# Local attention: where the mask is written and where the two parts of the rotation are summed

## The chip, the cores and the metric

The kernel runs on one core of a Trainium2 chip. The metric is the device time of one execution in microseconds (us). A core has TensorE (PE, matrix products), VectorE (DVE), ScalarE (ACT), GpSimd (POOL) and a queue for transfers (SP). Each works through its own instructions in order, and they wait for one another by semaphores.

## What is computed

The program is a stack of eight layers on a stream x of 8 x 256 tokens with 128 channels. The change is in the part called `ffn`, which stands in it twice. Each time it runs six pairs of a local attention and a gated feed-forward, so there are twelve local attentions. Cut to what matters:

```python
def attn_layer(x, Wqkv, qs, ksc, Wo):          # 16 heads of 64
    q, k, v = split(x @ Wqkv, 3)               # by heads
    q = l2norm(q) * qs;  k = l2norm(k) * ksc
    q = q * cos * scale + rotate_half(q) * sin * scale
    k = k * cos / scale + rotate_half(k) * sin / scale
    return local_attention(q, k, v) @ Wo
def local_attention(q, k, v):                  # windows of 32 queries
    sim = q @ concat(k_previous_window, k_own_window).T * 8
    sim = where(mask, -max, sim)               # 32 queries, 64 keys
    return softmax(sim) @ concat(v_previous_window, v_own_window)
```

The other layers of the stack (two attentions with other rules, a scan, a mixing layer) take the rest of the time; the change touches only names of semaphores there.

## The kernel before, in words

A local attention works on tiles of 128 tokens, 16 in a layer; two tiles are a unit (one sequence of 256 tokens), and a loop body has two units, so four tiles, tt = 0 to 3. Three bodies are a loop, the fourth is written out without the work for tiles that no longer exist. A layer starts with the projections of tiles 0 to 2 and the scores of tile 0.

All the order is written out by hand, one queue for each engine; in the body of tile tt each engine does work for tt and for the tiles ahead:

- **TensorE** (`fa_tensor`): products of x with `Wqkv` for tile tt+3, two banks at a time (L377), in turn with the transposes of q and k of tile tt+1 (`turn_qk`, L392 and L393): each 128x128 block is two transposing matmuls summed in PSUM, one of t1 (the cosine part) and one of t2 (the sine part), 32 a tile. Then the transposes of the probabilities of tt (L421), the first half of the scores of tt+1 (a bf16 matmul of the identity with the mask, L403, then 64 small matmuls on top of it, L408), the heads of tt (probabilities times values, 128 small matmuls, L434), the second half of the scores (again L403 and L408) and, in odd tiles, the projection by `Wo` (L446).
- **ScalarE** (`fa_scalar`): copies and squares of the banks of q, k and v (L499, L500, L502), the exponential of tile tt (`exps`, L525), the copies of the turned q and k (L520), then `rnorm` for tile tt+3 (L508, L510: one over the norm, by logarithm and exponential), the copy of the turned probabilities (`copy_probs`, L531), the copies of the heads (L539) and of the projection (L547). The copies of two banks of q and k stand ahead of the exponential, and `rnorm` stands ahead of `copy_probs`.
- **VectorE** (`fa_vector`): `softmax_norm` of tile tt (sum L600, reciprocal L602, product L606), `norms` of tile tt+3 (L611, L613), `unit_length` (L622, once for q, once for k: u = q or k over its norm), `softmax_shift` of tile tt+1 (maximum L592, difference L595), and in odd tiles the addition to the stream (L627).
- **GpSimd** (`fa_gpsimd`, `rotate`): for q and then for k, two half-width products of u with the sine table (L670, t2, the halves of each head swapped) and a product with the cosine table (L674, t1). It starts for a tile when the first L622 of that tile is done. t1 and t2 have two buffers each, by the parity of the tile.
- **SP** moves the values v into the layout of windows by small transfers.

What TensorE waits for in `heads`: the turned probabilities copied (L426). In `turn_qk`: both t1 and t2 of q (ahead of chunk 0) and of k (ahead of chunk 2), and a free bank. In `scores`: q and k copied out of PSUM, and the scores of the tile before read.

Of the kernel before, what the change touches and what calls it, by code (L numbers as in the profile page):

```python
# [8 lines left out]
BF16 = mybir.dt.bfloat16  # L9
ALU = mybir.AluOpType  # L10
# [104 lines left out]
def program(nc, d, out, parts=ALL):  # L115
    ctx = ExitStack()
    with ctx:
# [29 lines left out]
        ident_b = sb("ident_b", P, BF16)  # L147
        masks_b = sb("masks_b", 2 * 2 * WIN, BF16)
# [76 lines left out]
        masks_cast = sem("masks_cast")  # L225
# [141 lines left out]
        def fa_tensor(pe, run):  # L367
# [12 lines left out]
            def turn_qk(g, tt, chunks):  # L380
                t1, t2 = t1s[tt % 2], t2s[tt % 2]
                for c in chunks:
                    n = place_qk(tt, c)
                    pe.wait_ge(turned_copied, nth(g, TURN_PER, n))
                    if c % 2 == 0:
                        pe.wait_ge(t2_ready, nth(g, 2 * TILES, 2 * tt + c // 2) + 3)
                        pe.wait_ge(t1_ready, nth(g, 2 * TILES, 2 * tt + c // 2) + 3)
                    for j in range(4):

                        o = PS[:, TURN + n % 2, j * P:(j + 1) * P]  # L390
                        cols = slice((4 * c + j) * P, (4 * c + j + 1) * P)
                        pe.matmul(o, t1[:, cols], ident[:], start=True, stop=False, is_transpose=True)  # L392
                        last = pe.matmul(o, t2[:, cols], ident[:], start=False, stop=True, is_transpose=True)  # L393
                    last.then_inc(turned, 1)

            def scores(g, tt, s):
                uu, par = divmod(tt, 2)
                if s == 0:

                    wait_alone(pe, turned_copied, nth(g, TURN_PER, place_qk(tt, 3)) + 2)  # L400
                    wait_alone(pe, scores_read, nth(g, TILES, tt))
                mask = masks_b[:, par * 2 * WIN:(par + 1) * 2 * WIN].rearrange("p (o j) -> p o j", o=1)
                pe.matmul(PS[:, SCORE + s, :], ident_b[:], mask.broadcast_to([P, PAIRS, 2 * WIN]),  # L403
                          start=True, stop=False, skip_group_check=True)
# [74 lines left out]
        def fa_scalar(act, run):  # L479
# [46 lines left out]

            def copy_probs(g, tt, final):
# [21 lines left out]
            def body(g, it, final):  # L549
                for tt in range(TILES):  # L550
# [5 lines left out]
                    if ahead:  # L556
                        copy_turned(g, tt + 1, (0, 1))
# [16 lines left out]
            enter(1, 1)  # L574
            copy_qkv(first, 0, range(6), False)
# [8 lines left out]
            body(first + BODIES - 1, BODIES - 1, True)  # L584

        def fa_vector(dve, run):
# [36 lines left out]

            def add_stream(g, it, uu):
# [16 lines left out]
            for tt in range(3):  # L641
                norms(first, tt)
                unit_length(first, tt)
# [1597 lines left out]
```

## Time and profile before

| | before |
|---|---|
| times of three runs | 7197.66, 7207.6, 7215.52 us (median 7207.6) |
| profiled execution: own time, span | 7208.77 us, 7206.7 us |
| mean granted TensorE clock | 0.823 of full |
| busy: PE, DVE, ACT, POOL | 5312.7, 3840.9, 3985.0, 2396.7 us |
| L377 products with Wqkv (2304) | 1163.5 us busy |
| L408 scores, L434 heads (24576 each) | 451.1 and 534.7 us busy |
| L392, L393 transposes (6144 in all) | 1399.3 us busy, overlapping |
| L403 mask matmuls (384) | 149.3 us busy |
| L670, L674 products of GpSimd (768, 384) | 1152.7 and 938.5 us busy |

How to read it: the busy time of an engine is a sum over its instructions, and pipelined matmuls overlap, so the distance between the starts of two of them says more than the duration of one. The span runs from the first to the last instruction; the execution's own time holds 2.1 us more. Busy shares average over layers with different limits; within a stretch, the timeline shows which engine waits for which. An idle time in brackets stands behind the instruction that ended it, with its releaser. The local attentions lie between 873 and 3080 us and between 3947 and 6200 us of the span, in turn with their feed-forwards.

### The profile page before, as it was taken

The page shows a single profiled execution, that of the slowest core. Times are in us where ns is not written, and L with a number is a line of the kernel's source. Part 1 is how long each engine was busy: PE and PEld are TensorE (multiplying, and loading weights), DVE is VectorE, ACT ScalarE, POOL GpSimd, SP SyncE. Part 2 cuts the span into 40 slices and gives each one's busy share as a digit, 9 for nine tenths or more (in the row PEclk, how much of TensorE's full clock was granted, in tenths as well). Part 3 has the DMA queues.
Part 4 walks back from the last instruction along what each step waited for, and adds up shares of the span by engine and source line. Part 5 has one row for each costly group of instructions (what it writes and reads, how often), then busy time and mean ns, then how long its engine had stood idle before and what let it go on. Part 6 is the DMA issues. An engine that isn't in the chain of part 4 may idle for free. (4 is left out here: it accounts for less than half of the span.)

```text
span 7206.7 us, 178920 instructions
## 1 busy us (share of the span) xinstructions
PE 5312.7 (74%) x69288; PEld 3368.6 (47%) x69288; DVE 3840.9 (53%) x6202; ACT 3985.0 (55%) x8451; POOL 2396.7 (33%) x1351
## 2 busy tenths in 40 slices
PE   1000198888888888977777988888888979687778
PEld 0000065655656564733333655656564747343444
DVE  5555654645455554555554645455554546445854
ACT  4333264646455555539997646555554546355655
POOL 0000162626354444504443626354453535000000
PEclk6555599999999999976666989999998989766876
DMA  1000121212222121200000212212121212000000
GB/s 43 0 0 0 37 51 48 55 49 54 53 49 59 42 53 50 57 11 1 1 1 20 55 47 53 54 45 52 47 57 44 57 45 57 18 2 3 0 2 6
DMA packets 177838, 248.52 MB, mean 34 GB/s; under 512 B 51692, under 2 KB 79848, under 8 KB 175080
## 3 DMA queue, kind: packets, MB, share of 16 engines
q1 hardware_dynamic: 177128, 237.68, 13.2%
q8 instruction: 613, 10.04, 0.6%
q14 instruction: 97, 0.79, 0.0%
HBM read 43.50 MB, written 5.24 MB: 7 GB/s over the span
## 5 line engine op out<-in xcount | busy, mean ns | idle before, releaser
L377 PE MATMUL PS<-arena 128*128 128x512 f32 x2304 | 1163.5, 632 | 220.0 <-ACT arena L500 117.1
L670 POOL TENSOR_TENSOR arena<-arena 128x512 f32<-128x512 f32 x384 | 586.6, 1551 | 651.3 <-DVE arena L622 651.3
L670 POOL TENSOR_TENSOR lns<-arena 128x512 f32<-128x512 f32 x384 | 566.1, 1498 | 666.7 <-DVE arena L622 666.7
L377 PEld LDWEIGHTS PS<-arena 128*128 128x128 f32 x2304 | 412.9, 199 | 646.1 <-issue 359.7
L499 ACT ACTIVATE arena<-PS 128x512 f32<-128x512 f32 x768 | 472.1, 615 | 333.4 <-PE PS L377 258.4
L434 PE MATMUL PS<-arena 64*64 64x32 f32 x24576 | 534.7, 227 | 155.4 <-ACT arena L531 121.4
L592 DVE TENSOR_REDUCE arena<-PS 128x16 f32<-128x1024 f32 x192 | 235.2, 1225 | 731.0 <-PE PS L408 731.0
L1106 PE MATMUL PS<-arena 128*128 128x512 f32 x8 | 6.7, 1019 | 807.8 <-DVE arena L1040 807.8
L434 PEld LDWEIGHTS PS<-arena 64*64 64x64 f32 x24576 | 509.5, 141 | 191.7 <-issue 188.0
L611 DVE TENSOR_REDUCE arena<-arena 128x32 f32<-128x2048 f32 x192 | 438.8, 2285 | 293.4 <-ACT arena L500 286.1
L539 ACT ACTIVATE arena<-PS 128x512 f32<-128x512 f32 x384 | 208.9, 597 | 648.0 <-PE PS L434 648.0
L622 DVE TENSOR_TENSOR arena<-arena 128x1024 f32<-128x1024 f32 x384 | 471.7, 1270 | 148.4 <-ACT arena L510 148.4
L674 POOL TENSOR_TENSOR arena<-arena 128x1024 f32<-128x1024 f32 x192 | 482.3, 2512 | 0.0
L500 ACT ACTIVATE arena<-PS 128x512 f32<-128x512 f32 x768 | 476.4, 620 | 0.0
L408 PE MATMUL PS<-arena 64*32 64x64 f32 x24576 | 451.1, 218 | 31.3 <-issue 29.1
L520 ACT ACTIVATE arena<-PS 128x512 f32<-128x512 f32 x768 | 435.0, 634 | 49.7 <-PE PS L393 49.7
L2040 POOL TENSOR_TENSOR arena<-arena 128x1024 f32<-128x1024 f32 x128 | 297.9, 2356 | 477.6 <-ACT arena L1889 477.6
L674 POOL TENSOR_TENSOR lnc<-arena 128x1024 f32<-128x1024 f32 x192 | 456.2, 2376 | 0.0
L408 PEld LDWEIGHTS PS<-arena 64*32 64x32 f32 x24576 | 376.1, 107 | 148.7 <-issue 148.1
L1799 PE MATMUL PS<-arena 32*128 32x512 f32 x768 | 324.8, 968 | 163.6 <-DVE arena L1947 133.3
L600 DVE TENSOR_REDUCE arena<-arena 128x16 f32<-128x1024 f32 x192 | 234.3, 1220 | 316.2 <-ACT arena L525 316.2
L446 PE MATMUL PS<-arena 128*128 128x256 f32 x1536 | 385.5, 406 | 8.2 <-ACT arena L539 8.2
(254 smaller groups left out, 11101.2 us busy)
## 6 DMA issues: line engine op xcount, KB each, us to landing
arena<-arena SPq DMA_DIRECT2D x2880, 64.0 KB, 2.0
arena<-in_L_ffn_Wqkv SPq DMA_DIRECT2D x12, 1536.0 KB, 6.5
arena<-in_L_ffn_Wo SPq DMA_DIRECT2D x48, 128.0 KB, 6.3
scratch<-arena SPq DMA_DIRECT2D x4, 1024.0 KB, 4.8
arena<-scratch SPq DMA_DIRECT2D x4, 1024.0 KB, 7.6
arena<-in_L_ffn_W SPq DMA_DIRECT2D x12, 341.0 KB
arena<-in_ffn_scales SPq DMA_DIRECT2D x12, 128.0 KB, 5.8
arena<-in_L_ffn_W SPq DMA_DIRECT2D x12, 128.0 KB
```

Of the source, the lines that this page charges most:

```text
L377: pe.matmul(PS[:, QKV + n % 2, :], xs[uu % 2][:, par * P:(par + 1) * P], w, start=True, stop=True).then_inc(qkv_ready, 1)
L408: last = pe.matmul(PS[w * WIN:(w + 1) * WIN, SCORE + s, m * FD:(m + 1) * FD], qT[s * FD:(s + 1) * FD, m, w * WIN:(w + 1) * WIN], KT[uu % 2 ...
L434: last = pe.matmul(PS[(m % 2) * FD:(m % 2 + 1) * FD, HEAD + head_index(tt, s) % 2, at:at + WIN], VW[par][rows, w, m * FD:(m + 1) * FD], PT ...
L446: last = pe.matmul(PS[:, HEAD + n % 2, 0:T], Wo[:, m, :], AT[uu][:, m, :], start=(m == 0), stop=(m == PAIRS - 1))
L499: act.activation(chunk(raws[tt % 2], c), bank, ACT.Copy)
L500: act.activation(chunk(sq, c), bank, ACT.Square).then_inc(qkv_copied, 1)
L520: act.activation(to, PS[:, TURN + n % 2, :].rearrange("p (m t) -> p m t", m=4), ACT.Copy)\
L611: dve.tensor_reduce(nrm[:, 3, :], h3(sq), AX_X, ALU.add).then_inc(norm2_own, 1)
L622: dve.tensor_tensor(h3(raw[:, part]), h3(raw[:, part]), rn, ALU.mult).then_inc(u_ready, 1)
L670: last = pool.tensor_tensor(heads(t2)[:, :, a:a + 32], heads(raws[par])[:, :, b:b + 32], sine, ALU.mult)
L674: pool.tensor_tensor(heads(t1), heads(raws[par]), cosine, ALU.mult).then_inc(t1_ready, 1)
L1799: last = pe.matmul(PS[:, 2 * k + s, :], b0_KM[n % 2][rows_of(s), kt * P:(kt + 1) * P], b0_qb[(par + i // CHUNKS) % 2][rows_of(s), :, qt * ...
```

## The change

1. ScalarE writes the mask, broadcast over the 16 heads, into both score banks (`write_mask`, one activation of 128x1024) behind the exponential of the tile before; the scores are summed on top of it. The two mask matmuls of a tile and the bf16 copies of identity and mask go. At the start of a layer TensorE claims the two banks with one fp32 matmul each (`banks_marked`), and ScalarE waits for them.
2. The sine table holds its halves swapped, so GpSimd makes t2 with one full-width product per q and k instead of two halves. t2 now has its halves in u's order, and the swap is done where t1 and t2 are added.
3. t1 and t2 are added ahead of the transposes: q by VectorE (`rotate_q`, two additions of 128x512, of tile tt+2, between `softmax_norm` and `norms`), k by GpSimd (two additions of 128x512 behind its products, after a wait for them). TensorE transposes the sum: 16 single transposes a tile, after `q_rotated` and `k_rotated`.
4. In the first attention of the stack three semaphores are merged into others.

```diff
 def turn_qk(g, tt, chunks):
...
-                    if c % 2 == 0:
-                        pe.wait_ge(t2_ready, nth(g, 2 * TILES, 2 * tt + c // 2) + 3)
-                        pe.wait_ge(t1_ready, nth(g, 2 * TILES, 2 * tt + c // 2) + 3)
+                    if c == 0:
+                        pe.wait_ge(q_rotated, nth(g, TILES, tt))
+                    if c == 2:
+                        pe.wait_ge(k_rotated, nth(g, TILES, tt))
                     for j in range(4):
-                        pe.matmul(o, t1[:, cols], ident[:], start=True, stop=False, is_transpose=True)
-                        last = pe.matmul(o, t2[:, cols], ident[:], start=False, stop=True, is_transpose=True)
+                        last = pe.transpose(PS[:, TURN + n % 2, j * P:(j + 1) * P], t1[:, cols], ident[:])
 def scores(g, tt, s):
...
-                    wait_alone(pe, scores_read, nth(g, TILES, tt))
-                pe.matmul(PS[:, SCORE + s, :], ident_b[:], mask.broadcast_to([P, PAIRS, 2 * WIN]),
-                          start=True, stop=False, skip_group_check=True)
+                    wait_alone(pe, mask_ready, nth(g, TILES, tt))
 fa_tensor, ahead of the first qkv of a layer:
+            for s in range(2):
+                pe.matmul(PS[:, SCORE + s, :], ident[:], Wqkv[:, 0:CH], start=True, stop=True).then_inc(banks_marked, 1)
 fa_scalar:
+            def write_mask(g, tt):
+                S = PS[:, SCORE:SCORE + 2, :].rearrange("p s (m e) -> p (s m) e", e=FD)
+                act.activation(S, masks[:, tt % 2:tt % 2 + 1, :].broadcast_to([P, FH, 2 * WIN]), ACT.Copy)\
+                   .then_inc(mask_ready, 1)
...
                     exps(g, tt)
                     if ahead:
+                        write_mask(g, tt + 1)
                         copy_turned(g, tt + 1, (0, 1))
...
+            act.wait_ge(banks_marked, 2 * (run + 1))
+            write_mask(first, 0)
             copy_qkv(first, 0, range(6), False)
+        def add_halves(eng, t1, t2, k):
+            heads = lambda a: a[:, k * INNER:(k + 1) * INNER].rearrange("p (h e) -> p h e", e=FD)
+            for half in range(2):
+                a, b = half * 32, 32 - half * 32
+                last = eng.tensor_tensor(heads(t1)[:, :, a:a + 32], heads(t1)[:, :, a:a + 32],
+                                         heads(t2)[:, :, b:b + 32], ALU.add)
+            return last
 fa_vector:
+            def rotate_q(g, tt):
+                dve.wait_ge(t2_ready, nth(g, 2 * TILES, 2 * tt) + 3)
+                dve.wait_ge(t1_ready, nth(g, 2 * TILES, 2 * tt) + 3)
+                add_halves(dve, t1s[tt % 2], t2s[tt % 2], 0).then_inc(q_rotated, 1)
...
                     softmax_norm(g, tt, nth(g, TURN_PER, place_probs(tt - 1, 1, False)))
+                    if not (final and tt + 2 >= TILES):
+                        rotate_q(g, tt + 2)
                     if not (final and tt + 3 >= TILES):
                         norms(g, tt + 3)
                         unit_length(g, tt + 3)
...
             for tt in range(3):
                 norms(first, tt)
                 unit_length(first, tt)
+                if tt == 1:
+                    rotate_q(first, 0)
             softmax_shift(first, 0)
+            rotate_q(first, 1)
 fa_gpsimd, rotate (the table's halves are swapped where it is made):
-                    for half in range(2):
-                        a, b = half * 32, 32 - half * 32
-                        sine = table[:, 2 + k, par:par + 1, a:a + 32].broadcast_to([P, FH, 32])
-                        last = pool.tensor_tensor(heads(t2)[:, :, a:a + 32], heads(raws[par])[:, :, b:b + 32], sine,
-                                                  ALU.mult)
-                    last.then_inc(t2_ready, 1)
+                    sine = table[:, 2 + k, par:par + 1, :].broadcast_to([P, FH, FD])
+                    pool.tensor_tensor(heads(t2), heads(raws[par]), sine, ALU.mult).then_inc(t2_ready, 1)
...
+                wait_alone(pool, t2_ready, nth(g, 2 * TILES, 2 * tt + 1) + 3)
+                wait_alone(pool, t1_ready, nth(g, 2 * TILES, 2 * tt + 1) + 3)
+                add_halves(pool, t1s[par], t2s[par], 1).then_inc(k_rotated, 1)
```

## Rows read from the trace of the kernel before

**Rows 1.** Windows: an odd tile, then an even one; columns as in the first line.

```profile
core 0: us, PE busy (x) PEld busy (x) DVE busy (x) ACT busy (x) POOL busy (x), PEclk, DMA share, GB/s
1345.07:1365.04 19.97, 18.81 (x330) 14.14 (x327) 12.50 (x11) 11.12 (x22) 14.37 (x9) 1.00 0.26 62
1365.04:1381.12 16.08, 15.11 (x310) 11.13 (x311) 10.11 (x8) 11.44 (x23) 6.82 (x5) 1.00 0.22 53
```

**Rows 2.** Timeline of the even tile, TensorE: start, duration, instruction, idle before.

```profile
1365.04 1.98 PE L377 MATMUL PS<-arena 128*128 128x512 f32 x4 [0.49 <-issue]
...
1373.78 1.04 PE L421 MATMUL PS<-ident,arena 128*128 128x128 f32 x8
1374.66 0.38 PE L403 MATMUL PS<-masks_b,ident_b 128*128 128x512 bf16 x1
1374.97 1.10 PE L408 MATMUL PS<-arena 64*32 64x64 f32 x64
1376.61 2.52 PE L434 MATMUL PS<-arena 64*64 64x32 f32 x128 [0.55 <-ACT arena L531]
```

**Rows 3.** Waits: who, for whom, us in total, times, longest us.

```profile
PE PS L434 <- ACT arena L531: 121.4, 168, 1.6
```

**Rows 4.** Timeline of the even tile, ScalarE.

```profile
1368.12 1.08 ACT L525 ACTIVATE arena<-arena 128x1024 f32<-128x1024 f32 x1
...
1374.71 0.23 ACT L508 ACTIVATE arena<-arena 128x32 f32<-128x32 f32 x1
...
1375.20 1.06 ACT L531 ACTIVATE arena<-PS 128x512 f32<-128x512 f32 x2
```

**Rows 5.** Timeline, VectorE: L606 of the odd tile, then the even tile.

```profile
1351.04 1.30 DVE L606 TENSOR_TENSOR arena<-arena 128x1024 f32<-128x1024 f32 x1
...
1370.88 1.23 DVE L606 TENSOR_TENSOR arena<-arena 128x1024 f32<-128x1024 f32 x1
1372.17 2.29 DVE L611 TENSOR_REDUCE arena<-arena 128x32 f32<-128x2048 f32 x1
```

**Rows 6.** Groups by line (busy us, mean ns); last a single L670 in time.

```profile
L674 POOL TENSOR_TENSOR lnc<-arena 128x1024 f32<-128x1024 f32 x192 | 456.2, 2376 | 0.0
L333 DVE TENSOR_TENSOR XN<-lnc,lns 128x512 f32<-128x512 f32 x72 | 49.8, 692 | 45.1 <-ACT lns L324 45.1
...
1277.96 1.29 POOL L670 TENSOR_TENSOR lns<-arena 128x512 f32<-128x512 f32 x1
```

**Rows 7.** Timeline of a layer's start, VectorE and GpSimd, one instruction each.

```profile
1271.92 1.64 DVE L622 TENSOR_TENSOR arena<-arena 128x1024 f32<-128x1024 f32 x1 [0.65 <-ACT arena L510]
1272.44 2.27 POOL L670 TENSOR_TENSOR arena<-arena 128x512 f32<-128x512 f32 x1
1273.49 2.31 DVE L622 TENSOR_TENSOR arena<-arena 128x1024 f32<-128x1024 f32 x1
1274.68 3.32 POOL L674 TENSOR_TENSOR arena<-arena 128x1024 f32<-128x1024 f32 x1
```

**Rows 8.** Timeline, GpSimd: first and last products that run into the odd tile.

```profile
1340.65 3.42 POOL L670 TENSOR_TENSOR lns<-arena 128x512 f32<-128x512 f32 x2 [8.09 <-DVE arena L622]
...
1348.87 2.39 POOL L674 TENSOR_TENSOR lnc<-arena 128x1024 f32<-128x1024 f32 x1
```

**Rows 9.** Timeline of the same layer's start: TensorE, GpSimd, VectorE.

```profile
1253.79 4.58 PE L377 MATMUL PS<-arena 128*128 128x512 f32 x6 [8.39 <-issue]
...
1285.31 2.37 POOL L674 TENSOR_TENSOR lnc<-arena 128x1024 f32<-128x1024 f32 x1
...
1298.81 2.35 DVE L606 TENSOR_TENSOR arena<-arena 128x1024 f32<-128x1024 f32 x1
```

**Rows 10.** Two pauses of TensorE (timeline), and a window behind the second.

```profile
1562.29 4.28 PE L434 MATMUL PS<-arena 64*64 64x32 f32 x128 [0.97 <-ACT arena L531]
...
1587.88 4.51 PE L716 MATMUL PS<-XN,arena 128*128 128x512 f32 x6 [4.37 <-DVE XN L336]
...
1588.00:1589.00 1.00, 1.00 (x2) 0.43 (x3) 0.00 (x0) 0.00 (x0) 0.00 (x0) 0.71 0.00 0
```

More of the change, by code:

```diff
@@ L224, in program @@
         probs_ready = sem("probs_ready")
-        masks_cast = sem("masks_cast")
+        mask_ready = sem("mask_ready")
+        q_rotated = sem("q_rotated")
+        k_rotated = sem("k_rotated")
+        banks_marked = sem("banks_marked")
         vw_ready = [sem(f"vw_ready{i}") for i in range(2)]
@@ L380, in turn_qk @@
             def turn_qk(g, tt, chunks):
-                t1, t2 = t1s[tt % 2], t2s[tt % 2]
+                t1 = t1s[tt % 2]
                 for c in chunks:
@@ L651, in fa_gpsimd @@
             pool.wait_ge(attn_w_loaded, (run + 1) * ATTN_LOADS)
-            for k in range(4):
-                last = pool.tensor_tensor(table[:, k, :, :], rotary[:, k, :, :],
-                                          qks[:, k:k + 1, :].broadcast_to([P, 2, FD]), ALU.mult)
+            for k in range(2):
+                pool.tensor_tensor(table[:, k, :, :], rotary[:, k, :, :],
+                                   qks[:, k:k + 1, :].broadcast_to([P, 2, FD]), ALU.mult)
+            for k in range(2, 4):
+                for half in range(2):
+                    a, b = half * 32, 32 - half * 32
+                    last = pool.tensor_tensor(table[:, k, :, b:b + 32], rotary[:, k, :, a:a + 32],
+                                              qks[:, k:k + 1, a:a + 32].broadcast_to([P, 2, 32]), ALU.mult)
             last.then_inc(tables_ready, 1)
@@ L894, in program @@
         s_mix = sem("s_mix")
-        s_sh = sem("s_sh")
         s_rest = sem("s_rest")
@@ L937, in a0_sync @@
             sp.dma_start(a0_R.rearrange("p (b t) -> p b t", b=B), scratch[3].rearrange("b c t -> c b t"))\
-              .then_inc(s_backed, 16)
+              .then_inc(s_back, 16)
         def a0_vector(dve, n0):
@@ L947, in a0_vector @@
             dve.tensor_copy(a0_sh.rearrange("p (b t) -> p b t", t=T)[:, :, 1:T],
-                            XN[:].rearrange("p (b t) -> p b t", t=T)[:, :, 0:T - 1]).then_inc(s_sh, 1)
-            dve.wait_ge(s_sh, 1)
+                            XN[:].rearrange("p (b t) -> p b t", t=T)[:, :, 0:T - 1]).then_inc(s_rest, 1)
+            dve.wait_ge(s_rest, 3)
             for k in range(4):
@@ L1035, in a0_vector @@
                .then_inc(s_stat, 1)
-            dve.wait_ge(s_rstd, 2)
+            dve.wait_ge(s_rn, 4)
             dve.tensor_scalar(a0_tmp, a0_tmp, a0_small[:, 40:41], a0_small[:, 43:44], ALU.subtract, ALU.mult)\
                .then_inc(s_wkv, 1)
-            dve.wait_ge(s_backed, 16)
+            dve.wait_ge(s_back, 32)
             dve.tensor_scalar(a0_R, a0_R, a0_vec[:, 9:10], a0_vec[:, 10:11], ALU.mult, ALU.add).then_inc(s_gn, 1)
@@ L1088, in a0_scalar @@
             act.wait_ge(s_stat, 9)
-            act.activation(a0_small[:, 42:43], a0_small[:, 41:42], ACT.Ln, bias=eps[:, 0:1]).then_inc(s_rstd, 1)
-            act.wait_ge(s_rstd, 1)
-            act.activation(a0_small[:, 43:44], a0_small[:, 42:43], ACT.Exp, scale=-0.5).then_inc(s_rstd, 1)
+            act.activation(a0_small[:, 42:43], a0_small[:, 41:42], ACT.Ln, bias=eps[:, 0:1]).then_inc(s_rn, 1)
+            act.wait_ge(s_rn, 3)
+            act.activation(a0_small[:, 43:44], a0_small[:, 42:43], ACT.Exp, scale=-0.5).then_inc(s_rn, 1)
         def a0_tensor(pe, n0):
```

8 lines of the change are left out of this document (removed).

## The prediction

> **What bounds the kernel now.** I read the stretches by window first. The attention layers (12 of them, 16 tiles of 128 tokens each, 192 tiles) repeat a pair of tiles: an odd one, which also projects, of 19.97 us and an even one of 16.08 us, with TensorE busy 18.81 and 15.11 us of them at full clock [rows 1]. That looks like TensorE as the bound, and the change takes work from TensorE. So the question is what TensorE waits for in the rest. Its order of time for an even tile, counted as t from its first qkv matmul at 1365.04, shows one wait that counts: 0.55 us before the 128 head matmuls of L434, released by ScalarE's copy of the turned probabilities, L531 [rows 2]. The table of waits has the same pair 168 times in the 192 tiles [rows 3].
>
> Then I follow that wait back. L531 stands behind the two small activations of rnorm in ScalarE's own queue: L508 at 1374.71, L531 at 1375.20 [rows 4]. L508 needs the norms that VectorE makes with L611 (1372.17, 2.29 us), and L611 stands right behind L606 (1370.88, 1.23 us) with no idle time between them [rows 5]. L606 follows from the exponential, which ScalarE starts at 1368.12, after its four copies of the new qkv banks. So there is a ring: first qkv matmuls, copies, exponential (t = 3.1), sums and L606 (ends t = 7.1), L611 (ends t = 9.4), rnorm, L531, heads (t = 11.6), scores, next tile. VectorE and ScalarE set its length; the transposes of q and k lie beside it. TensorE has only 0.55 us of slack against it, and no piece of the ring has any.
>
> **The change part by part.**
>
> Transposes, 32 to 16. The eight transposes of L421 take 1373.78 to 1374.66, 0.11 us each, so 1.76 us of TensorE go per tile [rows 2]. They lie ahead of the wait at L434: worth nothing while the ring stands, since the wait grows by as much.
>
> Mask matmuls. Each holds TensorE 0.31 us (1374.66 to 1374.97) [rows 2]. The one of the first half lies ahead of the same wait, worth nothing. The one of the second half stands between heads and scores, on the ring: -0.3 us in every tile.
>
> The mask by ScalarE. No row shows a copy from SBUF to PSUM; the nearest is the exponential of the same 128x1024, 1.08 us [rows 4]. I take 1.1, bounds 0.9 and 1.4. It is queued behind the exponential and ahead of the copies of the turned q and k and of the next qkv banks, so TensorE gets its banks 1.1 us later. Today ScalarE goes from L502 into L508 with no idle time listed for L508 [rows 4], so this would be paid. It is hidden only because VectorE is later still (next item); if that cover were gone it would cost up to 1.1.
>
> VectorE's two additions for q. They come between L606 and L611, in the ring. A 128x512 with two SBUF inputs takes 0.69 us [rows 6]; the pair, overlapping a little, 1.35; bounds 1.2 without waits and, with a wait for a GpSimd instruction of 2.37 ahead of each, 6. Queued behind them are L611 and both L622, and ScalarE's L508 and L531 wait for L611.
>
> GpSimd. The two half-width sine products become one of 2.37 us, the duration of the cosine product, and two half-width additions of k of 1.29 are added [rows 6]: 4 x 2.37 + 2 x 1.29 = 12.1 us a tile where there were 2 x 2.37 + 4 x 1.29 = 9.9 without waits. Its throughput is enough (a pair of tiles has 36 us). But GpSimd and VectorE exclude each other. The rows of the prologue show it: L622 starts at 1271.92 and takes 1.64 instead of 1.23, because L670 is running; L670 then takes 2.27, the next L622 2.31, the next L674 3.32 [rows 7]. Each lasts its own time plus that of the other's: when both have work, they alternate, instruction by instruction.
>
> The Trainium skill (SBUF — State Buffer, "SBUF: two separate sides") says the same of the pair of ports that the two share, an exclusive lock for a whole instruction. It does not say who is next when both stand waiting; were VectorE always to keep the pair for its next instruction, the sum below would be that of the second case, 7400. The rows say alternate, so I go by them.
>
> Where they meet, **odd tile** (t from 1345.07): GpSimd's turn of a tile begins at 1340.65, and its last product, 1348.87 with 2.39, ends at 1351.26 [rows 8], just as L606 begins (1351.04, 1.30 long [rows 5]), t = 6.0 to 7.3. The cut of 0.2 to 0.4 in the sine products and the 0.3 that the next tile comes earlier cancel: the end of the last product stays at t = 6.1 to 6.3. From there GpSimd now has two additions. L606 runs first, to 7.3; addition one of k to 8.6; first half of q (waiting since 7.3) to 9.3; addition two of k to 10.5; second half of q to 11.2. L611 starts at 11.1 instead of 7.3: +3.8, -0.3 for the mask: +3.5 us.
>
> **Even tile:** GpSimd's turn begins at the same place of the tile ahead, but that tile is 3.9 us longer behind this place, for its projection [rows 1]. Without a meeting the turn ends at t = 6.2 + 2.6 = 8.8 in an odd tile, so here at 4.9, or 5.4 with the stream addition of VectorE in between; L606 starts at 5.8 [rows 5]. No meeting, by a margin of 0.4 us: +1.35 - 0.3 = +1.0.
>
> **Start of a layer.** Two fp32 matmuls that claim the score banks are put ahead of the first qkv. That stretch begins when weights and inputs are there, and six passes take 4.58 us, 0.76 each [rows 9]; four more are 3.1 us at that pace. A passage of the four products of one bank at full clock takes less (1.98 us for four [rows 2]), so an earlier start of TensorE may give part back: +2 (bounds 1 and 3.1). Then GpSimd, which works without a pause until 1287.7 (1285.31 plus 2.37) [rows 9] for two tiles, now needs 2 x 2.2 more for these and waits for the additions and L622s of VectorE that fall between (some 4.5, an estimate from their durations), and frees itself at about 1296.6. The addition for tile 1 stands ahead of the first softmax_norm and waits for GpSimd twice (+4); L606 of tile 0, which today takes 2.35 because of such a wait [rows 9], and the addition for tile 2 wait again (+4). I take +8 for the first tile, bounds +2 and +10.
>
> **Last three tiles** of a layer make no norms, so the ring isn't there; a mask matmul each: -1 in all.
>
> Sum for a layer: 2 + 8 + 6 x 1.0 + 6 x 3.5 - 1 = 36 us; 12 layers: 432. The renamed semaphores of the first attention and the two casts that go add nothing: they are the same waits under other names, and off the ring. The profiled execution took 7208.8 us (span 7206.7), 1 us over the median of the three runs, so 7208.8 + 432 = 7641; forecast 7640.
>
> **The rivals.**
>
> *Second case, the additions meet no GpSimd work, or VectorE goes first.* For it: in the even tile the two miss each other, and a shift of 1.5 us would do so in the odd one. Against: L606 already ends on GpSimd's last product. Each tile then +1.0, the first +3: 2 + 3 + 6 + 6 - 1 = 16 a layer, 192, so 7400.
>
> *Third case, the clock.* In an odd tile TensorE would stand idle some 4.5 us ahead of the heads. A pause of 4.37 us elsewhere was followed by a granted clock of 0.71 in the next microsecond, on the way from 2.4 to 1.2 GHz [rows 10]; after a longer one the heads took 4.28 us instead of 2.52 [rows 10, 2], 1.8 more, and the second scores and the projection follow at that clock. 1.7 to 4.8 us for 72 odd tiles: 7760 to 7985. Against: the clock is 1.00 through both tiles now [rows 1], and the pause lies between stretches of dense work. The Trainium skill (TensorE: Matmul & The Clock Gate, "Part 4: PE-mode transpose") has it that transposes don't count as activity for the clock gate; then the 16 that go cost no clock, and what is left of this case is the pause alone.
>
> *Fourth case, faster.* Place: the wait at L434. If it were not the ring that ends it, but a nearly finished TensorE, every tile would shrink by 1.76 + 0.62 = 2.38 us: 192 x 2.38 = 457, so 6752. It decides if the chain from the exponential to L531 has 1.35 us to spare. Against it: L606 and L611 touch, L508 comes 0.2 us after L611, L531 right behind. A part of it could give no change or a few per cent less.
>
> That the change doesn't do what it says is hardly possible: the instructions are written out one by one.
>
> **How the numbers follow.** Forecast 0.50 (7540 to 7760 by its bounds), second case 0.22 (7330 to 7540), third 0.17, fourth 0.08, and 0.03 for costs and gains that cancel. 7640 is the likeliest's own. The range 7330 to 7860 takes in the first two and the near half of the third. 0.3% is 22 us, about what a measurement can tell from no change; faster by more 0.08, within 0.03, slower by more 0.89.
>
> **What would show it.** Right: L611 starts 1.35 us or more behind the end of L606; the wait PE L434 behind ACT L531 grows from 0.55 to some 2 us in even and 4 to 5 in odd tiles; VectorE's additions and GpSimd's show durations well over 0.69 and 1.29 in odd tiles; tile pairs of 40 to 41 us instead of 36.05. Second case: pairs of 38. Wrong: pairs under 36, L434 without a wait. Third: granted clock under 1.00 in the middle of layers.

## The result, and the profile after

The changed kernel takes 7875.4 us (median of 4 runs, 7851.52 to 7899.01) where the kernel before takes 7211.56 on the same chips: a ratio of 1.0919 (95% interval 1.0876 to 1.0962). It is slower, by 664 us. The forecast was 7640 in a range of 7330 to 7860. The profiled execution has a span of 7897.2 us against 7206.7.

From the page of the changed kernel, busy times and then the granted clock in 40 slices (line numbers of the changed kernel from here on; the heads are L430 now, the scores L404, the products with `Wqkv` L378, the copy of the probabilities L536, the norms L628, `softmax_norm`'s product L623, the additions L599 on both engines):

```profile
PE 5524.5 (70%) x65880; PEld 3414.2 (43%) x65880; DVE 4239.3 (54%) x6586; ACT 4148.9 (53%) x8643; POOL 2883.4 (37%) x1371
...
PEclk5555787878788888886666877788887887766776
```

TensorE runs 3408 matmuls fewer and is busy for 212 us longer. The second line says why: most slices of the attention layers that had 9 before have 7 or 8 now. The windows of an even tile, the odd one behind it, and ten microseconds in the middle of that odd one:

```profile
1403.77:1420.76 16.99, 13.17 (x294) 8.84 (x292) 11.76 (x11) 12.56 (x25) 9.66 (x6) 1.00 0.20 50
1420.76:1447.42 26.66, 21.48 (x308) 16.00 (x309) 14.83 (x13) 11.58 (x22) 21.34 (x11) 0.81 0.23 54
1436.00:1446.00 10.00, 10.00 (x198) 8.87 (x195) 3.19 (x3) 1.09 (x2) 9.92 (x4) 0.51 0.17 39
```

Against [rows 1] the even tile is 0.9 us longer at full clock, and the odd one 6.7 us, with a stretch at half clock. TensorE in order of time through both:

```profile
1413.70 1.10 PE L404 MATMUL PS<-arena 64*32 64x64 f32 x64
1416.27 2.52 PE L430 MATMUL PS<-arena 64*64 64x32 f32 x128 [1.47 <-ACT arena L536]
...
1420.76 1.98 PE L378 MATMUL PS<-arena 128*128 128x512 f32 x4 [0.94 <-ACT arena L482]
...
1435.66 3.90 PE L430 MATMUL PS<-arena 64*64 64x32 f32 x128 [3.63 <-ACT arena L536]
1439.48 1.93 PE L404 MATMUL PS<-arena 64*32 64x64 f32 x64
1441.34 6.24 PE L442 MATMUL PS<-arena 128*128 128x256 f32 x16
```

The wait ahead of the heads was 0.55 us [rows 2]; it is 1.47 in the even and 3.63 in the odd tile. Behind the long one the clock falls, and the heads take 3.90 instead of 2.52, the scores 1.93 instead of 1.10, the projection 6.24 instead of 3.73 (both shorter durations stand in e2 below). The table of waits has 168 waits as in [rows 3], 2.6 times as long in all:

```profile
PE PS L430 <- ACT arena L536: 319.5, 168, 3.8
```

Why the odd tile's wait is long: VectorE first, one instruction each, then GpSimd.

```profile
1426.73 1.23 DVE L623 TENSOR_TENSOR arena<-arena 128x1024 f32<-128x1024 f32 x1
1427.87 1.76 DVE L599 TENSOR_TENSOR lnc<-lnc,lns 128x512 f32<-128x512 f32 x1
1429.55 1.76 DVE L599 TENSOR_TENSOR lnc<-lnc,lns 128x512 f32<-128x512 f32 x1
1431.24 2.27 DVE L628 TENSOR_REDUCE arena<-arena 128x32 f32<-128x2048 f32 x1
...
1426.72 2.36 POOL L599 TENSOR_TENSOR lnc<-lnc,lns 128x512 f32<-128x512 f32 x1 [0.17 <-POOL lnc L703]
1429.04 1.73 POOL L599 TENSOR_TENSOR lnc<-lnc,lns 128x512 f32<-128x512 f32 x1
```

The additions of VectorE need some 0.69 us each [rows 6] and last 1.76; those of GpSimd need 1.29 and last 2.36 and 1.73. They alternate as in [rows 7]: L623 holds GpSimd's first addition up, which holds VectorE's first one up, and so on. L628 starts at t = 10.5 where L611 started at 7.3.

In the even tile they don't meet. There L628 starts at t = 8.1, and one row of ScalarE shows how close a second bound is, the square of the last q and k bank, which L628 also needs:

```profile
1411.85 2.28 DVE L628 TENSOR_REDUCE arena<-arena 128x32 f32<-128x2048 f32 x1
...
1411.05 0.67 ACT L499 ACTIVATE arena<-PS 128x512 f32<-128x512 f32 x1
```

It ends at 1411.72, 0.1 us ahead of L628. ScalarE's queue has the mask in it, so without VectorE's additions, 1.3 us long, L628 could start only 0.1 us earlier.

The odd tile above is not the common one. The next pair of tiles in the same layer, heads of the even tile, VectorE's additions in the odd one, heads of the odd one:

```profile
1459.95 4.17 PE L430 MATMUL PS<-arena 64*64 64x32 f32 x128 [1.50 <-ACT arena L536]
...
1474.87 1.29 DVE L599 TENSOR_TENSOR lnc<-lnc,lns 128x512 f32<-128x512 f32 x2
...
1480.49 4.22 PE L430 MATMUL PS<-arena 64*64 64x32 f32 x128 [1.47 <-ACT arena L536]
```

Here the even tile's clock falls behind a wait of 1.50 us, and in the odd one the additions meet nothing, the wait is 1.47, and the clock falls all the same. Of the 72 odd tiles 28 stand behind an even tile at full clock: there the pair of additions takes 2.35 to 3.46 us, the wait is 3.16 to 3.76 us, and the clock falls in all 28. The other 44 stand behind a tile with a fall: the pair takes 1.29 us, the wait is 1.47 to 1.66, and the clock falls in 30 of them.

**Account by stage.** For each trace I took the 16 starts of the exponential in each of the 12 attention layers, and the time at the lower clock between the first and the thirteenth. A layer's start is counted from GpSimd's first product of the rotation's table, which waits for the layer's weights. Means of the 12 layers, in us:

| kernel | first table product to exp 0 | exp 0 to 1 | exp 1 to 12 | exp 12 to 15 | half clock, exp 0 to 12 |
|---|---|---|---|---|---|
| before | 47.5 | 18.2 | 198.4 | 46.4 | 2.8 |
| changed | 48.2 | 27.6 | 240.2 | 50.8 | 93.0 |
| e2, pause filled | 48.1 | 25.6 | 222.8 | 50.5 | 13.3 |
| e3, mask alone | 47.7 | 19.0 | 210.9 | 50.5 | 13.4 |
| e4, sums alone | 46.6 | 28.8 | 242.3 | 54.5 | 96.1 |
| e1, q behind norms | 48.3 | 24.0 | 215.4 | 50.2 | 34.6 |
| e9, as e1, mask by TensorE | 46.7 | 24.0 | 214.6 | 50.4 | 49.2 |
| e11, as e9, transposes twice | 48.1 | 24.0 | 199.9 | 45.7 | 10.9 |

The differences of the first two lines come to 0.7 + 9.4 + 41.8 + 4.4 = 56.3 us a layer, 676 us in all; the spans differ by 690.5. So nearly all of the loss is in the attention layers, and its largest part is in the repeated tiles.

And the same tiles split by whether any of their time, from exponential to exponential, was at the lower clock (number of tiles, median us; even tiles without the first of a layer):

| kernel | even, full | even, with a fall | odd, full | odd, with a fall |
|---|---|---|---|---|
| before | 60: 16.3 | none | 72: 19.5 | none |
| changed | 28: 17.3 | 32: 20.6 | 14: 20.4 | 58: 24.3 |
| e2 | 60: 17.2 | none | 69: 22.6 | 3: 24.7 |
| e3 | 49: 17.2 | 11: 19.9 | 58: 20.2 | 14: 22.2 |
| e1 | 38: 17.2 | 22: 20.1 | 58: 20.2 | 14: 22.6 |
| e9 | 32: 16.2 | 28: 19.4 | 37: 19.8 | 35: 23.5 |
| e11 | 60: 16.2 | none | 66: 19.4 | 6: 21.8 |

### The profile page after: what moved, and what is told of

It reads as the page before. It is cut to its first block and busy times, and to the rows that moved or that the text cites. A ratio compares the mean times of both kernels' runs of the same rounds, so it can differ in the third digit from the quotient of the medians.

```text
span 7897.2 us, 172940 instructions
## 1 busy us (share of the span) xinstructions
PE 5524.5 (70%) x65880; PEld 3414.2 (43%) x65880; DVE 4239.3 (54%) x6586; ACT 4148.9 (53%) x8643; POOL 2883.4 (37%) x1371
## 5 line engine op out<-in xcount | busy, mean ns | idle before, releaser
L378 PE MATMUL PS<-arena 128*128 128x512 f32 x2304 | 1259.0, 674 | 167.0 <-ACT arena L499 142.3
L430 PE MATMUL PS<-arena 64*64 64x32 f32 x24576 | 692.5, 265 | 330.6 <-ACT arena L536 319.5
L430 PEld LDWEIGHTS PS<-arena 64*64 64x64 f32 x24576 | 671.6, 184 | 361.1 <-issue 360.0
L701 POOL TENSOR_TENSOR lns<-arena 128x1024 f32<-128x1024 f32 x192 | 530.5, 2763 | 792.7 <-DVE arena L639 792.7
L701 POOL TENSOR_TENSOR arena<-arena 128x1024 f32<-128x1024 f32 x192 | 529.5, 2758 | 681.2 <-DVE arena L639 681.2
L378 PEld LDWEIGHTS PS<-arena 128*128 128x128 f32 x2304 | 421.9, 208 | 673.3 <-ACT arena L499 435.7
L639 DVE TENSOR_TENSOR arena<-arena 128x1024 f32<-128x1024 f32 x384 | 520.7, 1398 | 132.5 <-ACT arena L509 132.5
L1133 PE MATMUL PS<-arena 128*128 128x512 f32 x8 | 5.5, 846 | 807.4 <-DVE arena L1067 807.4
L404 PE MATMUL PS<-arena 64*32 64x64 f32 x24576 | 534.8, 249 | 28.5 <-issue 28.5
L628 DVE TENSOR_REDUCE arena<-arena 128x32 f32<-128x2048 f32 x192 | 437.5, 2278 | 210.9 <-ACT arena L499 210.9
L442 PE MATMUL PS<-arena 128*128 128x256 f32 x1536 | 521.9, 513 | 8.2 <-ACT arena L544 8.2
L404 PEld LDWEIGHTS PS<-arena 64*32 64x32 f32 x24576 | 460.2, 127 | 78.1 <-issue 67.9
L703 POOL TENSOR_TENSOR arena<-arena 128x1024 f32<-128x1024 f32 x192 | 477.7, 2488 | 0.0
L2067 POOL TENSOR_TENSOR arena<-arena 128x1024 f32<-128x1024 f32 x128 | 297.9, 2355 | 477.6 <-ACT arena L1916 477.6
L617 DVE TENSOR_REDUCE arena<-arena 128x16 f32<-128x1024 f32 x192 | 234.1, 1219 | 430.3 <-ACT arena L524 430.3
L442 PEld LDWEIGHTS PS<-arena 128*128 128x128 f32 x1536 | 401.0, 268 | 104.8 <-issue 10.8
```

What stands on the lines that cost most here:

```text
L378: pe.matmul(PS[:, QKV + n % 2, :], xs[uu % 2][:, par * P:(par + 1) * P], w, start=True, stop=True).then_inc(qkv_ready, 1)
L404: last = pe.matmul(PS[w * WIN:(w + 1) * WIN, SCORE + s, m * FD:(m + 1) * FD], qT[s * FD:(s + 1) * FD, m, w * WIN:(w + 1) * WIN], KT[uu % 2 ...
L430: last = pe.matmul(PS[(m % 2) * FD:(m % 2 + 1) * FD, HEAD + head_index(tt, s) % 2, at:at + WIN], VW[par][rows, w, m * FD:(m + 1) * FD], PT ...
L442: last = pe.matmul(PS[:, HEAD + n % 2, 0:T], Wo[:, m, :], AT[uu][:, m, :], start=(m == 0), stop=(m == PAIRS - 1))
L628: dve.tensor_reduce(nrm[:, 3, :], h3(sq), AX_X, ALU.add).then_inc(norm2_own, 1)
L639: dve.tensor_tensor(h3(raw[:, part]), h3(raw[:, part]), rn, ALU.mult).then_inc(u_ready, 1)
```

## The experiments

Each ratio is to the kernel before as it was timed beside that run: 7213.91 us for e1 to e4, 7224.15 for e5 to e8, 7239.97 for e9 and e10, 7211.09 for e11 and e12. Runs of different groups are compared by what each has over that time.

**e1: VectorE's additions behind the norms.**

```diff
 softmax_norm(g, tt, ...)
-if not (final and tt + 2 >= TILES): rotate_q(g, tt + 2)
 if not (final and tt + 3 >= TILES): norms(g, tt + 3)
+if not (final and tt + 2 >= TILES): rotate_q(g, tt + 2)
 if not (final and tt + 3 >= TILES): unit_length(g, tt + 3)
```

> The changed kernel with one move: VectorE adds the two parts of q behind norms instead of ahead of it, so the additions no longer stand between L606 and L611 of the ring (their names before), and lie beside ScalarE's two small activations. Theory of the ring: most of the loss goes, the pause of TensorE ahead of the heads falls from 1.5 and 3.6 us to about 1 in both kinds of tile, the clock stays at 1.00 in most tiles, and the time comes to 7200 to 7350. Rival, the sharing of the port counts wherever the additions stand (GpSimd is put behind, VectorE's difference and GpSimd's next tile too): 7550 to 7800.

Measured: 7572.47 us, ratio 1.0514 (1.0478 to 1.055). 303 us of the loss go by this one move, but the time is 222 us above the theory's upper end and in the rival's range, if not by the rival's cause. VectorE in an even tile:

```profile
1419.08 1.23 DVE L623 TENSOR_TENSOR arena<-arena 128x1024 f32<-128x1024 f32 x1
1421.32 2.29 DVE L628 TENSOR_REDUCE arena<-arena 128x32 f32<-128x2048 f32 x1 [1.01 <-ACT arena L499]
...
1423.82 1.30 DVE L599 TENSOR_TENSOR arena<-arena 128x512 f32<-128x512 f32 x2
```

The additions now run while ScalarE makes the reciprocal norm and last 1.30 us for both, without a meeting. But L628 doesn't follow L623: it waits 1.01 us for ScalarE's square. The odd tiles at full clock are 2.4 us shorter than in e2, the even ones are as long: another wait has taken the place. The clock falls in 36 of the tiles besides, and the wait ahead of the heads is 1.4 us in the median, where 1 was expected.

**e2: the pause filled.**

```diff
 def heads(g, tt, final):
+    pe.wait_ge(o_copied, nth(g, HEAD_PER, head_index(tt, 1)))
+    if not (final and tt > 0):
+        for _ in range(4 if par else 1):
+            pe.matmul(PS[:, HEAD + head_index(tt, 0) % 2, :], ident[:], Wqkv[:, 0:CH], start=True, stop=True)
     pe.wait_ge(turned_copied, nth(g, TURN_PER, place_probs(tt, 1, final)) + 2)
-    pe.wait_ge(o_copied, nth(g, HEAD_PER, head_index(tt, 1)))
```

> The changed kernel with filling work for TensorE ahead of the heads: 4 fp32 products of 128x512 in odd tiles, 1 in even ones, into a bank that the heads overwrite, ahead of the wait for the copied probabilities; nothing else waits for them. Theory that the fall of the clock in that pause costs about 300 us: the clock is 1.00 through the tiles, the heads take 2.5 instead of 3.9 us and the projection 3.7 instead of 6.2 in odd tiles, and the time falls to 7550 to 7650. Rival, the clock's fall costs little since TensorE waits anyhow: 7850 or more.

Measured: 7663.8 us, ratio 1.0623 (1.0605 to 1.064): 212 us less than the changed kernel, with more work, and 14 us above the theory's upper end. An odd tile, TensorE:

```profile
1487.17 3.70 PE L425 MATMUL PS<-arena,ident 128*128 128x512 f32 x8
1490.81 2.52 PE L433 MATMUL PS<-arena 64*64 64x32 f32 x128
...
1495.11 3.73 PE L445 MATMUL PS<-arena 128*128 128x256 f32 x16
```

Heads and projection are back at 2.52 and 3.73, and the odd tiles at 22.6 all but three. The time at the lower clock goes from 93.0 to 13.3 us a layer, 12.5 of them in its first tile. The four products take up the pause and don't lengthen it: from the start of the scores to that of the heads are 4.66 us, where the odd tile above has 4.73. So this is the changed kernel without its clock loss in the repeated tiles, and nearly the kernel that the prediction's sum described. The 212 us are a net figure: with no tile lengthened by the clock, VectorE's and GpSimd's additions meet in 67 of the 72 odd tiles, where they did in 28.

**e3: the mask by ScalarE alone**, in the kernel before (its `scores`, `write_mask` and the claiming products as in the change; t1 and t2 as before).

> The kernel before with the mask written by ScalarE alone (and the two claiming products at a layer's start); rotation and 32 transposes as before. Ring theory: ScalarE had no idle time ahead of L508 in even tiles, so its 1.06 us there are paid less the 0.3 of the mask product: +0.4 a tile on the mean, +2 a layer at the start, so 7270 to 7330. Rival, ScalarE had room and only the gain counts: -0.3 to -0.6 a tile, 7100 to 7190.

Measured: 7429.02 us, ratio 1.0296 (1.0279 to 1.0313). This part alone costs 215 us, more than either theory said. In an even tile, ScalarE and then VectorE (its norms are L617 here):

```profile
1365.79 1.02 ACT L527 ACTIVATE PS<-arena 128x1024 f32<-128x1024 f32 x1
...
1369.80 2.29 DVE L617 TENSOR_REDUCE arena<-arena 128x32 f32<-128x2048 f32 x1 [0.93 <-ACT arena L498]
```

1.02 us in ScalarE's queue arrive as 0.93 us of wait ahead of the norms. The even tiles are 17.2 us at full clock, as in the changed kernel, and the odd ones 20.2, 0.7 more than before. The rest is at a layer's end (+4.1 us) and in 25 tiles with a fall of the clock.

**e4: the sums alone**, the changed kernel with `scores`, the two mask products and the bf16 copies of the kernel before, and no `write_mask`.

> The changed kernel with the mask summed by TensorE as before (two bf16 products a tile, no claiming products, no mask by ScalarE): only the rotation's sums and the 16 transposes are changed. Theory: nearly all of the loss is here, since the additions stand in the ring and ScalarE's mask is covered by them: 7800 to 7900, with the clock falling as in the changed kernel. Rival, the mask by ScalarE carries a good part (it delays the copies for TensorE, and with them the pauses and the clock): 7450 to 7650.

Measured: 7911.86 us, ratio 1.0955 (1.0932 to 1.0977). This part alone costs 698 us, 12 us above the theory's upper end, so all of the loss is here too: the parts don't add up. At full clock its even tiles take 17.3 us. Each part alone lengthens the even tile by 0.9 to 1.0 us, and so do both together, since they are two ways to the same norms.

**e5: no additions by GpSimd.** k goes into the transposes without its sine part, and one filling product stands ahead of the heads in each tile.

```diff
-                add_halves(pool, t1s[par], t2s[par], 1).then_inc(k_rotated, 1)
+                pool.sem_inc(k_rotated, 1)
```

> The changed kernel without GpSimd's two additions of k (k goes into the transposes as its cosine part alone), and with one filling product of TensorE ahead of the heads in each tile, to keep the clock out of it. What the alternation of VectorE and GpSimd costs in odd tiles shows against the run with filled pauses (odd 22.83, even 17.16 us from exponential to exponential, 7664). Theory of the alternation: VectorE's additions for q take their own 1.3 us, the odd tiles fall to 20.3 to 20.8, the even ones stay at 17.2, the start of a layer gets shorter by about 5 us, and the time is 7350 to 7450. Rival, the odd tile's length comes from something other than GpSimd's additions (its longer products, or the banks that ScalarE hands over late): odd tiles over 22, 7600 or more.

Measured: 7487.77 us, ratio 1.0362 (1.0344 to 1.0379); odd tiles 20.5 us at full clock, by the theory, against 22.6 in e2. The time is 38 us above the theory's upper end. The start of a layer is some 3.5 us shorter than in e2, not 5, 13 even tiles have a fall, and the end of a layer takes 51.5 us. VectorE in an odd tile:

```profile
1498.90 1.23 DVE L625 TENSOR_TENSOR arena<-arena 128x1024 f32<-128x1024 f32 x1
1500.05 1.29 DVE L601 TENSOR_TENSOR lnc<-lnc,lns 128x512 f32<-128x512 f32 x2
1501.25 2.28 DVE L630 TENSOR_REDUCE arena<-arena 128x32 f32<-128x2048 f32 x1
```

1.29 us for both additions where the odd tile of the changed kernel has 3.44: the alternation costs 2.15 us of a tile in which all four additions meet.

**e6: rnorm late, in the kernel before.**

```diff
                         copy_qkv(g, tt + 3, (4, 5), True)
-                        rnorm(g, tt + 3)
                     copy_probs(g, tt, final)
+                    if further:
+                        rnorm(g, tt + 3)
```

> The kernel before with one move in ScalarE's order: rnorm stands behind the copy of the turned probabilities. Ring theory: L611 and the two small activations leave the ring, the wait before the heads falls from 0.55 to nearly nothing, and TensorE becomes the bound: 0.4 to 0.6 us less a tile, 7110 to 7150. Rival, TensorE was the bound already or GpSimd's later start gives it back: 7200 or more.

Measured: 7196.61 us, ratio 0.9963 (0.9949 to 0.9977). It is the only kernel of the study below the one before, by 27 us of the 60 to 110 expected. The wait ahead of the heads falls from 0.57 to 0.00 us in the median of the even tiles. Even tiles go from 16.3 to 15.9 us on the mean, the first of a layer from 18.2 to 16.4. The odd ones are at 19.2 where the clock stays full, but it falls in 11 of 72, so their mean stays at 19.5; a layer's end is 2.1 us longer.

**e7: sums, mask by TensorE, q behind norms, rnorm late.**

> Rotation summed ahead of 16 transposes, the mask by TensorE as before, VectorE's additions for q behind norms, and rnorm behind the copy of the turned probabilities. Ring theory: with the additions and the norms out of the ring the transposes taken away count at last: even tiles of 14.8 to 15.5 and odd ones of 17.5 to 18.5 us, 6900 to 7050 in all. Rival, GpSimd and VectorE share too much (they are busy for 13 to 14 us of a tile each, and alternate) or the clock falls since TensorE is less dense: 7150 or more.

Measured: 7334.87 us, ratio 1.0159 (1.0135 to 1.0183). The time is 285 us above the theory's upper end and in the rival's range. With a short ring the transposes do count in the best tiles (15.0 us even, 17.6 odd), but not in most. Two things are seen in the others. The clock falls in 24 of 60 even tiles. And TensorE has gaps inside one row of small matmuls that no engine releases:

```profile
1508.03 0.92 PE L435 MATMUL PS<-arena 64*64 64x32 f32 x32 [0.95 <-issue]
...
1528.33 0.42 PE L409 MATMUL PS<-arena 64*32 64x64 f32 x14 [0.87 <-issue]
```

**e8: as e7, with the mask by ScalarE.**

> As the run before, but with the mask by ScalarE, as in the changed kernel. ScalarE's 1.06 us stands ahead of the copies that TensorE waits for: theory, 0.3 to 0.9 us a tile more than with the mask by TensorE, so 7000 to 7200, and the last tiles of a layer longer by about 4 us together. Rival, once the ring is short the two mask products saved on TensorE outweigh it: below the run before by 20 us or more.

Measured: 7388.78 us, ratio 1.0236 (1.0216 to 1.0256), 54 us above e7 in medians: the mask by ScalarE costs even with a short ring, 0.28 us a tile, though less than in the kernel before. The absolute time missed the expectation as e7's did.

**e9: as e1, mask by TensorE.**

> Rotation summed ahead of 16 transposes, VectorE's additions for q behind norms, mask by TensorE as before: the run with the additions behind norms (7572), less the mask by ScalarE. That run's tiles had the length of the run with the mask alone (even 17.16 and odd 19.4 us at full clock). Theory: two things each lengthen the even tile by 0.9 us, ScalarE's mask and VectorE's additions ahead of the norms; with both gone the tiles are 16.3 and 19.5 as in the kernel before, what is left is the start of a layer (+5 us) and some falls of the clock: 7270 to 7400. Rival, the mask isn't what lengthens the tiles there, but GpSimd's additions are: 7500 or more.

Measured: 7520.3 us, ratio 1.0388 (1.0368 to 1.0408). Its tiles at full clock are nearly as the theory said: 16.2 and 19.8, where the kernel before has 16.3 and 19.5. Its time is in the rival's range; it has 280 us over the kernel before. The difference is the clock: 49.2 us a layer at half. The wait ahead of the heads is the same one, but longer: 1.17 us in the median of the even tiles and 1.24 in the odd ones, where the kernel before has 0.57 and 0.67. TensorE has less to do and comes to it earlier.

**e10: as e1, one filling product ahead of the heads.**

> The changed kernel with VectorE's additions behind norms (7572) and one filling product of TensorE ahead of the heads in each tile. Theory of the clock: the tiles at half clock (34.6 us of a layer's first 13 tiles) come back to full, 7400 to 7480. Rival, what is left over the kernel before is no matter of the clock: 7540 or more.

Measured: 7527.16 us, ratio 1.0405 (1.0379 to 1.0431), 45 us less than e1 (71 less by what each has over its kernel before), in neither expectation. Inconclusive: one product took the time at half clock to 15.2 us a layer, and the odd tiles grew by 0.3 us.

**e11: as e9, each of the 16 transposes issued twice.**

```diff
                     for j in range(4):
                         cols = slice((4 * c + j) * P, (4 * c + j + 1) * P)
-                        last = pe.transpose(PS[:, TURN + n % 2, j * P:(j + 1) * P], t1[:, cols], ident[:])
+                        for _ in range(2):
+                            last = pe.transpose(PS[:, TURN + n % 2, j * P:(j + 1) * P], t1[:, cols], ident[:])
```

> As the run with sums, mask by TensorE and additions behind norms (7520), but each of the 16 transposes is issued twice, so TensorE has the 32 transposes of the kernel before and only idle filling has changed. Theory that the clock falls because TensorE lost the 1.75 us of work: the falls, 49 us of a layer's first 13 tiles there, go back to under 10, the tiles are 16.3 and 19.6 us, and the time is 7280 to 7350, although TensorE does more. Rival, the transposes don't count for the clock, or the work taken away is not its cause: 7480 or more.

Measured: 7310.14 us, ratio 1.0153 (1.0126 to 1.018). 16 transposes more in each tile make the kernel 210 us faster, 181 of them by what each has over its kernel before (280 and 99). The windows from the second to the thirteenth exponential of the second layer, of e9, of e11 and of the kernel before:

```profile
1345.57:1555.77 210.20, 187.43 (x3331) 129.10 (x3330) 135.76 (x127) 122.19 (x247) 145.81 (x68) 0.93 0.23 55
```

```profile
1324.29:1520.48 196.19, 186.34 (x3507) 139.94 (x3506) 129.99 (x127) 123.73 (x247) 148.14 (x68) 1.00 0.25 59
```

```profile
1313.25:1510.35 197.10, 187.23 (x3507) 140.43 (x3506) 122.83 (x105) 123.78 (x247) 119.75 (x68) 1.00 0.24 59
```

With the same 3507 matmuls the repeated tiles take the same time as before the change, although VectorE and GpSimd do the additions. With 176 fewer (the 16 in each of 11 tiles) the clock is 0.93 on the mean and the stretch 14 us longer. The wait ahead of the heads is 0.54 us in the median of the even tiles, 1.17 in e9. The Trainium skill (TensorE: Matmul & The Clock Gate, "Part 4: PE-mode transpose") says, beside durations of bf16 transposes, that full clock doesn't engage for transpose mode, which doesn't count as busy in the same way. Here 128x128 fp32 transposes kept the clock up: of the two kernels only their number differs. Each transpose is a weight load and a product, and no run separates the two.

What is left of e11 over the kernel before, 99 us, is for the most part a layer's start: 0.6 + 5.8 us, 77 us in twelve layers. The clock still falls in every first tile, 8.9 of the 10.9 us.

**e12: the changed kernel, each transpose issued twice.**

> The changed kernel with each of its 16 transposes issued twice. If TensorE's missing transposes carry the clock's fall here too: the pause ahead of the heads in odd tiles shrinks from 3.6 to about 2 us and the falls get rarer, 7680 to 7780. Rival, the pause alone carries it and transposes count for nothing: 7850 or more.

Measured: 7803.19 us, ratio 1.0825 (1.0793 to 1.0858). 72 us less than the changed kernel, 23 above the expected range. The falls in even tiles go from 32 to 18; in odd ones they stay, 60 of 72. In 42 of these, behind an even tile at full clock, the pause is 3.23 to 3.55 us, not the 2 expected: there it is enough for a fall with 32 transposes in the tile too. In the other 18 the wait is 1.35 us in the median.

## Why the prediction was wrong

The direction was right and the size was not. The step that failed is the clock: the sum takes every tile at full clock and so puts the clock's cost at nothing, and the third case, which prices it, has a chance of 0.17 in a range that ends at 7860. The runs show 212 us in its place: by so much the changed kernel is above e2, which does the same work and more with the clock kept up. The ground against the third case was that the clock was 1.00 through both tiles before and that the pause lies between stretches of dense work. But the clock of the kernel before says nothing of a kernel whose TensorE waits.

The third case had the right event, but its mechanism was not whole either, and that its 7760 to 7985 holds the measured time is in part luck. It had a pause of some 4.5 us in all 72 odd tiles. A pause of 3.16 to 3.76 us stands in 28 of them, and the clock fell in each. It fell as well in 30 odd and 32 of 60 even tiles with a wait of only some 1.5 us, and in every first tile. In the profiled executions, whose spans differ by 247 us, the even tiles are 113 us longer in all than in e2, the odd ones 97, the first ones 24. In the odd ones two things work against each other: a fall costs 3.8 us (24.2 against 20.4 behind a tile with a fall), and the long tile ahead saves the meeting of the additions (20.4 against 22.6).

*What bounds the kernel.* Right. VectorE and ScalarE set the length, TensorE waited beside them: e1, which changes nothing but VectorE's order, gives 303 us back (with the meetings and most falls of the clock gone too), and e6 takes the norms out of the ring and has no wait left ahead of the heads.

*The transposes are worth nothing.* Right for the ring (e9), wrong for the clock: taking them away costs 181 us between e9 and e11. The prediction let the third case be the pause alone: by the Trainium skill (TensorE: Matmul & The Clock Gate, "Part 4: PE-mode transpose") the transposes taken away cost no clock.

*VectorE's additions.* Right. 1.29 us for a pair that meets nothing, 3.44 for one that meets both of GpSimd's (2.36 for one that meets one of them); e5 and e1 each remove the meeting. In the odd tile with the meeting L628 came at t = 10.5 where 11.1 was forecast: the four turns took 3.4 us behind the end of L623, not 3.9. But the meeting was forecast for all 72 odd tiles and stands in 28 of the changed kernel, for the clock had lengthened the tile ahead of the others.

*Tiles at full clock.* The forecast was +1.0 and +3.5. e2 has 17.2 and 22.6, which is +0.9 and +3.1, a pair of 39.8 us where 40 to 41 were forecast.

*The mask by ScalarE.* The cover that was named is real and thin: 0.1 us in the even tile. That it would be paid without this cover, at up to 1.1 us, is what e1 shows, at 1.01. Two errors: the alone price of this part was not 0.4 a tile (an expectation of e3, not of the prediction), and at a layer's end, where the prediction had -1, it costs: e3 is 4.1 us longer from exponential 12 to 15, by 1.2 to 1.6 in each of the three tiles. That there is no norm there to hide the queue of ScalarE is a reading of mine, not tested. Nor is the mask the only thing that lengthens the end: e9, with the mask by TensorE, takes 50.4 us with 17.6 at the lower clock, the kernel before 46.4 with 4.4, e11 45.7 with 2.1. How much of the changed kernel's 50.8 (24.2 at the lower clock) is which stays open.

*A layer's start.* Forecast +2 and +8; e2 has +0.5 and +7.4. The +2 for the claiming products left out what the start gains: e9, without them and with half the transposes, is 0.8 us below the kernel before, and e1, with them and the mask by ScalarE, 1.6 above e9. The waits are those foretold, but the clock fell in all twelve first tiles of e2 as well, so its +7.4 isn't the waits alone. VectorE's rows of the changed kernel, both L639 of tile 1, the additions for tile 1 and those for tile 2:

```profile
1335.95 5.98 DVE L639 TENSOR_TENSOR arena<-arena 128x1024 f32<-128x1024 f32 x2 [0.65 <-ACT arena L509]
...
1358.90 5.63 DVE L599 TENSOR_TENSOR lnc<-lnc,lns 128x512 f32<-128x512 f32 x2
...
1367.76 4.57 DVE L599 TENSOR_TENSOR arena<-arena 128x512 f32<-128x512 f32 x2
```

*The sum.* 36 us a layer were forecast; e2, the changed kernel at nearly full clock, has 0.5 + 7.4 + 24.4 + 4.1 = 36.4, and 7664 us against the 7640 forecast. The other 212 us are the clock. That the sum comes out so near is in part luck: 2, 26 and 0 were forecast for the terms of 0.5, 24.4 and 4.1.

*The rivals.* The second case (no meeting, 7400) is refuted by e2, where the additions meet in 67 of 72 odd tiles; in the changed kernel they miss each other in 44, but only behind tiles that the clock had lengthened. The fourth (faster, 6752) is refuted by all of them; even with the ring shortened, e7 came to 7335.

Not settled: why the tiles with a fall, in e9 and in the changed kernel with waits of 1.5 us, are those and not others. Not tried: a start of a layer in which the additions don't stand ahead of the first `softmax_norm`, the most likely way to bring e11 to the kernel before.

## What to carry to other kernels

When the engine with the largest busy share is also waiting, follow the wait back: work taken from the engine that waits buys nothing, and work put between two touching instructions of the chain is paid in full, plus whatever it now collides with. Before taking work off TensorE, ask what its clock does in the kernel that results; here a fall of the clock cost 3.3 us of an even and 3.8 of an odd tile where the edit's own price in the chain was 0.9 and 3.1, and issuing useless transposes was faster than leaving them out. And test a pair of edits one by one: here each alone lengthened the even tile by 0.9 to 1.0 us, and both together no more than that.

## What the runs showed of the hardware that I had not expected

- fp32 transposes keep TensorE's clock up: 16 more in a tile of 16 us took the time at half clock from 49.2 to 10.9 us a layer and what the kernel has over the one before from 280 to 99 us (e9, e11).
- In the changed kernel the clock fell behind all 28 pauses of 3.16 to 3.76 us, but also in 62 of the 104 tiles with a wait of some 1.5 us. There a tile with a fall takes 3.3 us (even) and 3.8 us (odd, behind a tile with a fall) more than one without; over the kernels of the table the medians differ by 2.0 to 3.9.
- A long tile lets GpSimd finish ahead of the next one: behind tiles with a fall the 14 odd tiles at full clock take 20.4 us, not e2's 22.6. The clock's loss and the loss by the meeting of VectorE and GpSimd therefore don't add up.
- Gaps of over 0.8 us that no engine releases stand inside TensorE's rows of small matmuls. In heads and scores the kernel before has 17 of them, e7 58. Ahead of each of the 75, less than 2 us before it or in it, a packet of the DMA queue of kind "instruction" starts; a stretch of that length taken at random has one in about a third of the cases. So the loading of instructions is a likely cause; no run varied it.
